# A third residual buffer, a fifth transposed context, and a new order of steps in a fused eight-batch transformer kernel

## The reference

```python
x = x + L0_xattn(ln(x), ctx, ctx)     # 16 heads of 16, softmax
x = x + L0_ffn(ln(x))                 # gate picks one of 8 experts per token (argmax), plus identity
x = x + L1_xattn(ln(x), ctx)          # 16 heads of 16, softmax under a fixed mask
x = x + L1_ffn(ln(x))                 # 3 cycles: out += coupling(out) * twist(out)
x = x + L2_xattn(ln(x), ctx, ctx)     # sigmoid features, running sum over tokens
x = x + L2_ffn(ln(x))                 # linear layer plus the 2 best of 8 low-rank experts
x = x + L3_xattn(ln(x), ctx, ctx, m)  # one head of 256, softmax
x = x + L3_ffn(ln(x))                 # silu(x Wg) * (x Wu), then Wd; integer weights / 127
```

## Time and profile before

| | |
|---|---|
| runs | 986.34, 987.83, 988.33 us |
| median | 987.83 us |
| span of the profiled execution | 986.1 us |
| busy: TensorE, VectorE, ScalarE, GpSimd | 949.3, 634.1, 536.3, 221.5 us |
| mean granted TensorE clock | 0.993 |

### The profile page before, as it was taken

How to read it: one execution, slowest core, us unless ns; L and a number is a source line. 1 busy time by engine, 2 the same in 40 slices (tenths; PEclk the granted TensorE clock), 3 DMA queues, 4 the chain that set the end, 5 groups by cost and what they waited for, 6 DMA issues and landing times.

```text
span 986.1 us, 17493 instructions
## 1 busy us (share of the span) xinstructions
PE 949.3 (96%) x6126; PEld 702.7 (71%) x6126; DVE 634.1 (64%) x2245; ACT 536.3 (54%) x1097; POOL 221.5 (22%) x317
## 2 busy tenths in 40 slices
PE   8999999989999999999999999999999999999998
PEld 6665665757687766778687766776686757777777
DVE  4634674675675776867586776775776676736564
ACT  1341644776368643875448644866376544864421
POOL 3104311303240132403141023302321032012210
PEclk9999999999999999999999999999999999999999
DMA  7308535400540023520432104402132004000000
GB/s 261 58 30 226 127 113 113 88 10 17 113 94 9 11 50 70 113 49 13 80 73 46 44 1 86 98 11 49 27 67 59 12 17 92 1 12 1 1 1 22
DMA packets 41078, 58.27 MB, mean 59 GB/s; under 512 B 4096, under 2 KB 35840, under 8 KB 37376
## 3 DMA queue, kind: packets, MB, share of 16 engines
q1 hardware_dynamic: 39600, 48.59, 23.6%
q10 hardware_dynamic: 1392, 8.56, 2.3%
HBM read 41.67 MB, written 13.89 MB: 56 GB/s over the span
## 4 chain that ended last, share of the span: by engine, by line
PE 77%; ACT 9%; DVE 8%; issue 4%; POOL 1%; DMA 1%; ACTq 0%; SPq 0%; DVEq 0%; POOLq 0%
PE bank L1657 11%; PE bank L1984 6%; PE bank L1517 6%; PE bank L1736 6%; PE bank L1714 6%; PE bank L1508 6%; PE bank L1629 4%; PE bank L1995 4%; PE bank L1771 4%; PE bank L1765 3%; PE bank L1717 3%; ACT PT L886 2%; ACT QA L873 2%; PE bank L1797 2%; PE bank L1526 2%
## 5 line engine op out<-in xcount | busy, mean ns | idle before, releaser
L886 ACT ACTIVATE PT<-bank 128x512 f32<-128x512 f32 x256 | 153.0, 598 | 127.4 <-PE bank L1717 71.8
L1657 PE MATMUL bank<-w,xhT 128*128 128x512 f32 x256 | 126.8, 599 | 0.0
L1714 PE MATMUL bank<-QA,KA 104*128 104x256 bf16 x512 | 112.7, 273 | 12.4 <-ACT PT L886 10.5
L1184 DVE CUSTOM_DVE_ANT_0 bank<-bank,maskb 128x256 f32<-128x256 f32 x256 | 101.7, 450 | 25.7 <-PE bank L1629 25.4
L1177 DVE TENSOR_REDUCE mx<-bank 128x2 f32<-128x512 f32 x128 | 83.6, 684 | 28.9 <-PE bank L1629 28.5
L1629 PE MATMUL bank<-KA,QA 96*128 96x256 bf16 x512 | 91.1, 273 | 1.9 <-DVE mx L1184 0.8
L1984 PE MATMUL bank<-xhBT,wi 128*128 128x256 f32 x336 | 87.0, 390 | 2.9 <-DVE hT L1491 2.5
L1714 PEld LDWEIGHTS bank<-QA,KA 104*128 104x128 bf16 x512 | 46.5, 99 | 60.3 <-issue 45.8
L1230 DVE SCALAR_TENSOR_TENSOR x<-bank,one,x 128x256 f32<-128x256 f32 x128 | 61.5, 481 | 21.6 <-PE bank L1657 17.6
L873 ACT COPY QA<-bank 8x256 bf16<-8x256 bf16 (+1 forms) x128 | 67.8, 575 | 10.1 <-PE bank L1695 8.8
L1984 PEld LDWEIGHTS bank<-xhBT,wi 128*128 128x128 f32 x336 | 59.2, 191 | 12.9 <-DVE hT L1491 5.6
(11 more groups left out here) (311 smaller groups left out, 2028.3 us busy)
## 6 DMA issues: line engine op xcount, KB each, us to landing
QA<-scratch SPq DMA_DIRECT2D x90, 128.0 KB, 4.8
scratch<-kparts SPq DMA_DIRECT2D x30, 192.0 KB, 2.4
KA<-scratch SPq DMA_DIRECT2D x15, 384.0 KB, 4.6
scratch<-qparts SPq DMA_DIRECT2D x30, 192.0 KB, 2.3
KA<-scratch SPq DMA_DIRECT2D x15, 256.0 KB, 5.5
w<-pack ACTq DMA_DIRECT2D x1, 2345.0 KB, 8.3
wi<-ipack ACTq DMA_DIRECT2D x1, 2304.0 KB, 8.5
xin<-x_in SPq DMA_DIRECT2D x8, 256.0 KB, 6.3
```

The costliest lines, as they stand in the source:

```text
L886: act.activation(PT[:, n % RING, :, :].rearrange("p t s -> p (t s)"), st_bank[:, :], ACT.Exp).then_inc(exp_s, 1)
L1184: last = dve.tensor_tensor_reduce(s, s, maskb[:, t, :], op0=ALU.add, op1=ALU.max, scale=1.0, scalar=-HUGE, accum_out=mx[:, i % 4, n % GH, ...
L1657: last = pe.matmul(bank[n % 2][:, :], xhT[:, kk, t * P:(t + 1) * P], W("exp0", KT)[:, kk, i * 512:(i + 1) * 512], start=(kk == 0), stop=(k ...
L1714: last = pe.matmul(st_bank[:, t * S:(t + 1) * S], KA[m][0:KM, v, t * P:(t + 1) * P], QA[m][0:KM, v, :], start=True, stop=(m == 0))
```

## The change

- `CTX` is 5: a fourth tile of its own in the ring of transposed contexts, and SyncE's load of a batch waits for the batch five before. Batch 7's `sg`, `p3T` and `twT` then stand in `ctxT3` in place of `ctxT0`.
- `XB` has three buffers (`NX`), and VectorE waits for the store of the batch three before. Each edit takes 2 KB more of a partition.
- All five strings of `TURNS` are new. On VectorE, ScalarE, GpSimd and SyncE they hold the same steps in another order. TensorE's holds 11 letters w in place of 106, and 16 z in place of 54. So there are 266 matmuls of L2004 fewer in the program (35 calls of `spin` in place of 168), and all other instructions are the same in number and shape.

```diff
-CTX = 4
+CTX = 5
+NX = 3
 TURNS = {
     "tensor":
-        "pppwwwppwwwwwwwwwwwwwwwwppwwwwwwwwwwwwpwwwwwpwpwwwwwwppwwwwwwwwwwwwwwwwwwwsswwspspssvsvswwvsvpsvswwv"
+        "ppppppwwwppwpwwpppwsspsspsvssvwssvvssvspsvsvpvvwpvssvvvvvvpvwvvvvpvvvvpvvpvvwppspssssssssssssssssspp"
...
-        XB = [sb(f"XB{i}", [P, T, D]) for i in range(2)]
+        XB = [sb(f"XB{i}", [P, T, D]) for i in range(NX)]
...
-                        if b >= 2:
-                            dve.wait_ge(stored, nth(stored, b - 2, 16))
-                        update(XB[b % 2], ot_bank, xb1, added)
+                        if b >= NX:
+                            dve.wait_ge(stored, nth(stored, b - NX, 16))
+                        update(XB[b % NX], ot_bank, xb1, added)
```

More of the change, by code:

```diff
@@ L95 @@
[L95 to L96 removed]
+        "ppppppppsspspppssppssppssspsppppsapspsspppspssasaaapbbpbpsbbaappsspbbspsppaappasbsbsbbpbsasbappspbsp"
+        "ppsassaasbbpbppbbpsspbaassppsppasasapbsbbbbbppsbsasasppsppppbpsaaapssbbpbbabsabsssppssssaapbabbpssbs"
+        "sbabbabsaaababaababaaaaababcccccccccccbccc",
     "scalar":
[L98 removed]
@@ new lines @@
+        "pppppppppppvvpvvvpvvvvvvpvvvvvvvvvvvpvpssspppbssbppvvbvvvvpvvsvvvpvvvvvvvvvvvvpbbbvvpvvvsvvbvvbvvvvv"
+        "vvvbvvvvbbvvppspasbaavavavvvbvavpvvvpvapbavvvvvpvavvvabvbvabbbbpvapavavasvvvvvvvvavabvvpvvvbvvbvvvvb"
+        "vpsbpsabbaavabavbvvavpbpvabvpvvvvbavbvvvvabvavvvavvpavaabavvvvvavavvpvvpvvsvbvvbvvvvbvvvbvbpbspapsaa"
+        "bavvabvvvpbvpvavvbvavbavpbvvvvbaavpvavvvavaavabpvpvvavvavsvvvbvbvpvvbvpvvvvbvvvbvbpvssbabppabavbavbv"
+        "vvapbvvavbvvvavaavvvvavbvpavvvvavaapavvpvvvvavavsvvbvpbvvvvbvvvvbvvbvbvsppsbababavavabvvvavpvpvvvbva"
@@ new lines @@
+        "vpbvvvvvabapvavvvavavbaaavvsvvvvvavvvvavvvvvvvbvvbvvbpvpbabbsasabpabvvabvvvpvpbvvvvvbvavvvvvbvvavbva"
+        "vaavvvavvvbvpsaaaavvvvvpaavvvvvbvbvsvvsvbvvcbabbaavavbavvvbavvbvabvavbavbavvvavvbvavaavavvbvaavbaaba"
+        "aaaaabaaaaaaaaaaabaaaaaaaaaaabbaaaabbccccbbcbcbcbccccccccccccccccccc",
+    "vector":
+        "ppppppppvpppvppvpssssssssssssssssssssvvpvpvpvspspsssssssssssppssssssssssspssssbsssssssssvsssssssvpvs"
+        "vspspssvssssssssspsvsvssvpvsssvasasssssspssssasaassssspspssbssssssssvssssssvsaaaspvsvppssvssspspaaas"
+        "asaasasabbssvbbbbsbvbbsvssvbsbbvaabsppssssbbssbssssaaabspbsbssssssbsssbsssssvbssvsaaabvvssssvaaasaas"
+        "absbpasppsssabsbsbbsvbsbbbsbsspbbsvbvspvsbsvasabbbssspsssssspsabssasabsspsbssssbssbsbsssvaassasssvss"
+        "svssbvspaaapasvpsasbsappsbaabsbsbbsbbbbbsbvbsbssbvvsvssbsbvabppassbsssssbssspbssbsssabaasssbssssssss"
+        "sbssavssvaassspvpvssbsvpaaaaassasssbapabpsbsbsbbbbbbsvbsbsbvssbvsvsbsbvabasbsspsssbspssssaaassbpssss"
+        "sssbsssbsssvssbssssssasasavbvsvsssvsasaaaabasssbaabsvbspvbbbpbbbbvsvpsbbvabasbssspbpbbssssssbsssssas"
+        "basassbssspssbvbsssssbssvsvvsssaaasvssssbssssssbssaaasaasasabssabsbssvbsbvbbbbbpvvbbbvaabsscssbsbssb"
+        "sssaaasbssssbbssbssabsaabvvbaaaaaavbvababvabaacabbbbbbbaaaabbbaaaabaaaaaaaaaabbaabacacccbcccccbccccc"
+        "bccccbcccccbcbccccccccccccccccbcccccc",
@@ L575, in last @@
                     sp.wait_ge(final.s["xb_new"], at(final, "xb_new", b, 3, h))
-                    sp.dma_start(out[b, lo * P:hi * P].rearrange("(t p) d -> p t d", p=P), XB[b % 2][:, lo:hi, :]
+                    sp.dma_start(out[b, lo * P:hi * P].rearrange("(t p) d -> p t d", p=P), XB[b % NX][:, lo:hi, :]
                                  ).then_inc(stored, 16)
@@ L588, in rest @@
                     sp.wait_ge(xb_new, nth(xb_new, b, 3))
-                    sp.dma_start(out[b].rearrange("(t p) d -> p t d", p=P), XB[b % 2][:, :, :]).then_inc(stored, 16)
+                    sp.dma_start(out[b].rearrange("(t p) d -> p t d", p=P), XB[b % NX][:, :, :]).then_inc(stored, 16)
                     yield
@@ L710, in net @@
                     for h, lo, hi in parts(b):
-                        plus(o2, XB[b % 2], "bao", xba_s, lo, hi)
+                        plus(o2, XB[b % NX], "bao", xba_s, lo, hi)
                         yield
@@ L729, in rest @@
                             pool.wait_ge(dn_ps, nth(dn_ps, b - 1, 1))
-                        plus(L.xbB, XB[b % 2], "blin", L.s["xbb_s"], lo, hi)
+                        plus(L.xbB, XB[b % NX], "blin", L.s["xbb_s"], lo, hi)
                         yield
@@ L1327, in net @@
                 for b in range(B):
-                    xl = XB[b % 2]
+                    xl = XB[b % NX]
                     dve.wait_ge(added, PLACE[b, 1] + 1)
```

53 lines of the change are left out of this document (17 added, 36 removed).

## The result

The changed kernel is slower: 990.92 us median of 17 runs (986.66 to 1000.62) against 986.11 us (983.97 to 990.21) for the kernel before, measured anew beside it in 17 runs; the ratio is 1.0049, with a 95% interval of 1.0029 to 1.0069. Forecast were 983.3 us and a range up to 990.0. The profiled execution took 992.97 us with a span of 991.2.

The account below looks back on a forecast made before the run. TensorE's work plus its holes was taken to bound the kernel. Terms of 0, +0.5, -1.3, -1.8, -2.0, 0 and 0 made -4.6 against 986.1: a span of 981.5, a median near 983.3 us, range 978.0 to 990.0.

Parts of the forecast that it names:

- the order's terms: At 92 to 101, 101 to 219 and 738 us: the new order was to give -1.3, -1.8 and -2.0 us.
- Fillers at the start: Before first scores: cutting 38 fillers to 2 gains 1.3 us, offset by L1257 and a dip; 0, between -1.3 and +2.5.
- fillers in batch 0's scores: Between first L1629 and first L1657: 62 fillers cut to 8, only clock at risk; +0.5 us, bounds 0 and 3.6.
- the clock takes it back, and more: Rival: losing 266 fillers lowers the clock at start, batch 0's scores and tail; about +3.5, or 991 us; chance 0.19.
- 92 to 101 us: TensorE ahead of L1526: half of L1517 fills the 1.32 us wait; -1.3 us, bounds 0 and -2.7.
- 101 to 219 us: Batches 0 and 1: L761 moves into ScalarE's idle time, holes and a dip shrink; -1.8 us, bounds -6 and +3.
- 738 us: Stall at 738 to 748 us: a pair ahead of updates L1318 keeps TensorE supplied; -2.0 us, bounds -3.7 and 0.
- The new order blocks: Rival: a step too early in SyncE's or GpSimd's queue delays splits or loads; 987 us; 0.24 together with "nothing happens".
- No order of steps can take much out of that half: From 237.4 to 738 us: TensorE busy 496.27 of 500.60 us at full clock; middle stretches unchanged to 1 us.
- The tail: From 891.6 us on: earlier L1822 gives -1.5, lost fillers' dips +1.5; sum 0, bounds -3 and +3.

Follow-up runs that it names:

- refill: The changed kernel with 274 of before's 336 fillers put back ahead of the same steps: 987.21 us, 1.0002 of before.
- best1: The changed kernel with the edits of fill_early, fill_tail and loadback: 985.80 us, 0.9981 of before.
- fill_early: The changed kernel with before's fillers up to batch 0's experts only, 16 in place of 38 ahead of the first scores: 986.59 us, 1.0007 of before.
- before_cut: The kernel before with 12 in place of 38 fillers ahead of the first scores: 987.02 us, 0.9998 of before.
- sync_only: The changed kernel with SyncE's last two of six query loads L494 issued with the other four, ahead of key stores and loads: 989.52 us, 1.0017 of before.
- best3: best2 with the same step of SyncE moved as in sync_only: 980.73 us, 0.9940 of before.
- fill_tail: The changed kernel with before's 108 fillers in the tail and its own 38 ahead of the tail: 992.47 us, 1.0058 of before.
- best2: best1 with half of batch 2's context projection L1508 moved behind two heads of batch 1's first scores: 984.39 us, 0.9977 of before.
- bare: The kernel before with its own order and buffers, but only the changed kernel's 70 fillers: 997.75 us, 1.0126 of before.
- loadback: The changed kernel with ScalarE's load of the last weights (L757) issued behind copy L810 again: 991.50 us, 1.0051 of before.
- fill_start: The changed kernel with before's fillers ahead of the first scores only, 16 in place of 38: 987.53 us, 1.0009 of before.

## Why the prediction was wrong

The sum said -4.6 us and the medians show +4.8, 9.4 us apart. About 4 us of that are the fillers' price, and the rest are the 5.1 us that the order's terms (-1.3, -1.8, -2.0) had promised: with the fillers in place the new order is level with the old one (refill, 1.0002, 0.9984 to 1.0021), or 0.2% ahead of it with 16 fillers ahead of the first scores (best1). Refill's profile shows where its gains go: 4.9 us less in the middle and 2.2 us less up to batch 6's layer-1 scores, but 2.4 us more up to batch 0's experts and 4.2 us more from there to batch 1's.

- **The clock (the step that failed first).** "Fillers at the start" was put at 0 and "fillers in batch 0's scores" at +0.5 us. Both together cost 4 us (fill_early against the change, 1.0007 to 1.0049), within the upper ends that I had given, 2.5 and 3.6, but eight times the +0.5 of the sum. I took the fillers' cover to be the waits in which they stood, and so their going to be free; what they held up was the clock of the dense work behind the waits. I reasoned that TensorE "has real work in most of this stretch"; the profile shows it cold twice, on L1736 and L1517. The rival "the clock takes it back, and more" was the case that came. It had 0.19. That its 991 us meet the measured 990.92 is luck: it added up +6, with a share for the tail, whose fillers cost nothing, and -2.5 of gains, of which with the fillers in place nothing can be measured. The Trainium skill, "TensorE: Matmul & The Clock Gate", section "Why this matters for your kernels", asks for short idle gaps between bursts of matmuls, and so spoke against taking the fillers out. The trace agrees, with a mean clock of 0.972 without them and 0.995 with them in the same order (refill), and it deserved more than a rival's chance. The argument against that rival, that the middle holds its clock without fillers, was read from one execution of the old order; in four of the twelve profiles of the new order the clock falls in the middle too (see the last section).
- **The start.** -1.3 for the 38 fillers: the scores did start at 34.08 in place of 35.32 us in the kernel after, yet cutting those fillers alone gained nothing (before_cut), where the load itself held the scores until 34.76 us. That L1257 comes into the way of L1560 was seen, and refill's chain shows it with its 2.29 us.
- **92 to 101 us (the order's terms, second step that failed).** Forecast -1.3, measured +3.6. L1526 has no idle of 1.32 us ahead of it, as said. But the order shown above the prediction has L1508 on `ctxT` ahead of the first L1629, and the prediction looked at the two other moves alone. What a moved step waits for, and what is queued behind it, was asked for L1517 and not for this one.
- **101 to 219 us.** Forecast -1.8; the stretch up to batch 2's experts is 2.0 us shorter. The size fits in this one profile, and that is luck: the other profiles of the new order take 134.5 to 140.6 us there, those of the old order 134.3 to 135.9. A gain isn't shown.
- **738 us.** Forecast -2.0. The stall went as said (0.34 us for L1318, no idle for hT), but a wait of 2.59 us and a fall of the clock came in front of the scores 15 us later, so the stretch gained 0.9 and the one behind it, where the fall lies, lost 2.3. "The new order blocks" named this mechanism, with SyncE's queue and 3.7 us beside the gains; I gave it no term in the sum. With the two issues moved (sync_only, best3) the stretch takes 27.9 and 27.5 us, so then more than the forecast's 2.0 is gained.
- **The middle.** "No order of steps can take much out of that half" was wrong: 4.9 us went from 488.2. Busy shares hid them. For the same matmuls (some 2,800) between batch 2's and batch 6's experts the two kernels show

```profile
237.40:675.50 438.10, 433.98 (x2798) 323.94 (x2797) 305.59 (x1081) 265.84 (x523) 109.01 (x148) 1.00 0.27 56
```

```profile
245.10:679.00 433.90, 431.36 (x2799) 322.47 (x2798) 302.78 (x1083) 266.05 (x523) 109.84 (x151) 1.00 0.26 56
```

  so only 1.6 of the 4.2 us saved are idle time (4.1 against 2.5); the rest was inside "busy". A matmul's row lasts from its start to its end, longer than the distance to the next one when they follow closely (0.27 against 0.11 us for L1714), so by these two numbers a wait of up to some 0.15 us (an estimate) leaves no idle time. Starts show it. Take for each matmul the distance to the next start, and as the usual one the median for the same pair of lines: what exceeds it by over 0.1 us comes to 31.8 us in 170 places before and 28.4 us in 152 after, 3.4 of the 4.2 us.
- **The tail.** Forecast 0, measured +0.9 in one profile, and its fillers are worth nothing (fill_tail). Right in the sum; that the reordered net gains 1.5 there and lost fillers cost 1.5 isn't shown, and fill_tail speaks against the second.

## What to carry to other kernels

Matmuls whose result nobody reads are not free to remove just because they stand in waits: ask at what clock the dense work behind the wait runs, and try their removal by itself. When an order of steps changes, list every step that now stands ahead of another one's data, DMA issues above all, and look for the new wait in the stretch behind the one that was mended; here one such pair of issues hid a part of what the new order had won. Where an engine is 99% busy, measure starts, not busy time, before calling it full. And before a stretch of a single profile is called a loss or a gain, look for it in the profiles of other kernels that share its order.

## What the runs showed of the hardware

The spread of one kernel's runs goes with the clock. best2's twelve runs go from 980.58 us at a mean granted clock of 0.997 to 990.77 us at 0.986, best3's six from 980.33 at 0.998 to 985.26 at 0.991: 0.7 to 0.9 us for each 0.001. The changed kernel's 17 runs have clocks of 0.969 to 0.979 and spread over 14 us, those of before over 6. That the missing fillers make it less steady as well as slower is likely but not shown: bare, without them, spreads over 6 us in six runs, and fill_early, with the early ones, over nearly 12 in twelve. A single profiled execution tells where a dip can come, not how often it comes.

The clock also falls in the middle, where TensorE has hardly a hole. best1, loadback, fill_start and sync_only, four of the twelve profiled kernels of the new order, have one such fall of 6.8 us between 562.8 and 574.0 us, none of the four of the old order has. In best1 TensorE had idled 0.41 and 0.46 us shortly before it, up to 560.87 and 561.61 us, and was never idle within it:

```profile
562.80:569.60 6.80, 6.80 (x28) 5.46 (x28) 4.21 (x19) 2.59 (x7) 0.90 (x2) 0.50 0.01 2
```

These are the four whose middle takes 3 us longer than that of the other eight. So a busy share near 100% does not say that the clock will hold.
